# The last group's fourth maximum subtracted on TensorE, and a residual sum with a block maximum one tile later in the fill

## What is computed

```
x = x + attention(ctx, layernorm(x))          # 8 heads of 16; softmax over 64 keys
x = x + ffn(layernorm(x))                     # h = silu(xq @ Wg) * (xq @ Wu);  y = hq @ Wd
```

## Time and profile before

| | |
|---|---|
| median of 3 runs | 199.22 us (198.94 to 199.98) |
| the profiled execution, its own time | 199.67 us |
| its span, first to last instruction | 197.9 us (1.77 us lie around it) |
| busy in the span | PE 183.7, DVE 177.3, POOL 142.0, ACT 132.2 us |
| attention part | up to about 112 us |
| fill, tiles 0 to 7 | about 112 to 130 us |
| steady loop | about 130 to 187 us |
| drain | 187 to 197.9 us |

### The profile page before, as it was taken

One profiled execution on the slowest core, in us unless ns is written; L12 is line 12 of the kernel. 1 busy time (PEld: TensorE's weight loads), 2 busy tenths in 40 slices (PEclk: granted clock), 3 DMA queues, 4 the chain that ended last, 5 costly groups with the idle time before them and its releaser, 6 DMA issues.

```text
span 197.9 us, 5833 instructions
## 1 busy us (share of the span) xinstructions
PE 183.7 (93%) x2097; PEld 141.2 (71%) x2097; DVE 177.3 (90%) x394; ACT 132.2 (67%) x281; POOL 142.0 (72%) x208
## 2 busy tenths in 40 slices
PE   5979999999899999999998999789999998999884
PEld 5546876859659688597785776467778686778783
DVE  6539997899999999999979998999999989999971
ACT  3046999959769699696877846385476473766661
POOL 6333785566697897984928496797999975877891
PEclk9999999999999999999999999999999999999999
DMA  5799990400200000000000000000101010101005
GB/s 192 239 246 298 387 296 15 158 6 19 91 3 2 3 3 3 2 0 5 3 3 0 5 0 0 0 5 2 53 0 53 3 53 0 53 5 55 0 0 164
DMA packets 13699, 12.00 MB, mean 61 GB/s; under 512 B 790, under 2 KB 10590, under 8 KB 13670
## 3 DMA queue, kind: packets, MB, share of 16 engines
q1 hardware_dynamic: 13086, 11.23, 18.1%
q10 hardware_dynamic: 584, 0.39, 0.6%
HBM read 9.52 MB, written 2.10 MB: 59 GB/s over the span
## 4 chain that ended last, share of the span: by engine, by line
PE 55%; POOL 17%; issue 11%; DVE 7%; DMA 4%; ACT 2%; SPq 1%; POOLq 0%; DVEq 0%; ACTq 0%
PE bank L1065 7%; PE bank L1156 5%; PE bank L1053 5%; POOL wq_y L397 5%; DMA x_all<-in_x 4%; POOL hq L412 3%; PE bank L1028 3%; PE bank L1124 3%; PE bank L1121 3%; PE bank L1016 3%; PE a_pair L1016 3%; PE bank L1136 3%; PE bank L1002 3%; PE bank L1059 3%; POOL xn L284 2%
## 5 line engine op out<-in xcount | busy, mean ns | idle before, releaser
L1156 PE MATMUL bank<-wdT,hT 128*128 128x128 f32 x186 | 26.4, 278 | 1.8 <-issue 0.8
L1121 PE MATMUL bank<-guT,xqT 128*128 128x352 f32 x64 | 24.5, 464 | 1.8 <-DVE hh L875 1.8
L1156 PEld LDWEIGHTS bank<-wdT,hT 128*128 128x128 f32 x186 | 23.2, 191 | 3.1 <-issue 1.9
L1124 PE MATMUL bank<-guT,xqT 128*128 128x352 f32 x64 | 24.2, 460 | 0.0
L412 POOL TENSOR_TENSOR hq<-wq_u,sch 128x704 f32<-128x704 f32 x15 | 21.2, 1413 | 3.6 <-DVE wq_u L901 3.5
L397 POOL TENSOR_TENSOR wq_y<-hh,ivh 128x704 f32<-128x704 f32 x15 | 21.1, 1409 | 2.9 <-ACT ivh L632 2.3
L737 DVE TENSOR_REDUCE den<-prob 128x8 f32<-128x512 f32 x32 | 19.8, 663 | 0.0
L626 ACT COPY hT<-bank 128x384 f32<-128x384 f32 x32 | 15.2, 474 | 5.1 <-PE bank L1136 5.1
L1065 PE MATMUL bank<-wsT,cT 128*128 128x128 f32 x128 | 17.2, 278 | 0.1
L1136 PEld LDWEIGHTS bank<-ident,hq 128*128 128x128 f32 x96 | 11.9, 141 | 7.4 <-issue 3.0
L1136 PE MATMUL bank<-ident,hq 128*128 128x128 f32 x96 | 15.8, 274 | 1.5 <-POOL hq L412 0.9
(11 more groups left out here) (138 smaller groups left out, 506.0 us busy)
## 6 DMA issues: line engine op xcount, KB each, us to landing
cT<-in_ctxT SPq DMA_DIRECT2D x8, 512.0 KB, 5.4
x_all<-in_x SPq DMA_DIRECT2D x8, 256.0 KB, 6.4
mask_bc<-in_mask_rows SPq DMA_DIRECT2D x8, 256.0 KB, 6.5
out_y<-mask_bc SPq DMA_DIRECT2D x7, 256.0 KB, 2.2
wsT<-in_WsT ACTq DMA_DIRECT2D x1, 256.0 KB, 5.0
out_y<-mask_bc SPq DMA_DIRECT2D x1, 192.0 KB, 2.0
w_all<-in_wg SPq DMA_DIRECT2D x1, 176.0 KB
w_all<-in_wu SPq DMA_DIRECT2D x1, 176.0 KB
```

The lines of the kernel that those rows point to most:

```text
L1121: nc.tensor.matmul(gu_bank[2 * n % 3][:, 0:I], xqT[g % 2][:, t], guT[:, 0, :], start=True, stop=True).then_inc(pe_g, 1)
L1124: nc.tensor.matmul(gu_bank[(2 * n + 1) % 3][:, 0:I], xqT[g % 2][:, t], guT[:, 1, :], start=True, stop=True).then_inc(pe_u, 1)
L1156: last = nc.tensor.matmul(bank[:, j * P:(j + 1) * P], hT[n % 2][:, c, :], wdT[:, c, :], start=(c == 0), stop=(c == 2))
```

## The change

Three edits. In the last group (step k = 8) pair 3 is treated as the other pairs: TensorE subtracts its maxima in the bank with one more product behind that of pair 2, VectorE's subtraction is gone, and `exp` waits for `pe_mm` and reads the bank. And `x2_add(7)` with `block_max(6)` moves on VectorE from m = 4 to m = 5, behind that m's h_product(5), h_max(2) and h_reciprocal(2).

```diff
 exp(g, p):
-                if p == SUB:
+                if p == SUB and g < NG - 1:
                     act.wait_ge(sub_ok, g + 1)
                     nc.scalar.activation(pr, pr, ACT.Exp, scale=float(HD) ** -0.5).then_inc(p_ok, 1)
                     return
 VectorE, attn_step(k):
-                if on(g2):
+                if on(g2) and k < NG:
                     minus_max(g2)
                 if on(g4):
                     block_max(g4)
 VectorE, loop over m:
-                if m == 4:
+                if m == 5:
                     x2_add(NG - 1)
                     block_max(NG - 2)
 TensorE, attn_step(k):
                     minus_max(g2, 2)
+                    if k == NG:
+                        minus_max(g2, SUB)
                     prob_transpose(g2, 0)
                     prob_transpose(g2, 1)
```

## The result

| | before | changed |
|---|---|---|
| median | 199.22 us (10 runs, 198.75 to 200.64) | 201.66 us (10 runs, 200.28 to 203.38) |
| the profiled execution, its own time | 199.67 us | 201.09 us |
| its span | 197.9 us | 198.6 us |
| mean granted clock in the span | 1.000 | 0.991 |

What follows compares the result with a forecast made beforehand. The prediction took VectorE to set the pace from the end of the fill through half the steady loop. Its terms, 0 + 1.32 + 0.60 = 1.92 us, added to 199.22 gave 201.1 us, range 199.5 to 202.0.

Steps and rivals of the forecast that it cites:

- The first edit at zero: Last group's fourth maximum subtracted on TensorE: gain at the end taken as 0, capped at 0.06 us by h_product(1).
- block_max(6) 1.86 us late through GpSimd's queue: block_max(6) ends 1.86 us later, so GpSimd's scales, hq_unit(0), h_scales(2) and y_unit(2) all come 1.86 us later.
- 1.32 us at h_product(8): On VectorE at tile 8: silu(8) comes 1.86 us late, 0.57 us is slack, so h_product(8) starts 1.32 us later.
- TensorE's lateness as harmless: TensorE, 1.86 us late at h_transpose(0), has room to fall back into step with VectorE over the next tiles.
- 0.60 us at s3_round(6): VectorE arrives at 135.39 us while GpSimd's hq_unit(2) runs until 135.99, and waits the full overlap, 0.60 us.
- They follow each other without a gap: GpSimd's scales, hq_unit(0), h_scales(2) and y_unit(2) run back to back, so all are 1.86 us later.
- The row at 162.03: s3_round(7)'s second instruction in the kernel before: 1.76 us against a median of 0.72, blocked by an hq_unit until 163.23.
- The clock as a rival at 0.06: TensorE's clock falls to 1.2 GHz after some 3.4 us idle before h_transpose(0), giving 203.6 us; chance 0.06.
- The price of 2.5 us: Extra loss beyond the forecast if TensorE's clock falls: two tiles at half speed, about 2.5 us.
- The sum: Total delay on VectorE: 0 + 1.32 + 0.60 = 1.92 us, giving 201.1 us, 1.0% slower.
- the meeting: VectorE's s3_round(6) and GpSimd's hq_unit(2) overlap near 135 us and lock each other out, costing 0.60 us.
- VectorE as the bound: From 120.73 to 158.66 us VectorE, busy 37.13 of 37.93 us, sets the pace; delaying it delays the end.

Runs made afterwards that it cites:

- second measurement: The changed kernel timed once more, on the chip of its version with 26 useless products in TensorE's wait: ratio 1.0084 to the kernel before, median 201.59 us.
- e4_bmax_later: The kernel before with only block_max(6) moved to m = 5, x2_add(7) staying at m = 4: ratio 1.0120, or 2.4 us slower.
- e3_x2_later: The kernel before with only x2_add(7) moved to m = 5, block_max(6) staying at m = 4: ratio 1.0028.
- e6_after_scales: The changed kernel with GpSimd's scales2_of(6), which waits for block_max(6), put behind hq_unit(0), h_scales(2) and y_unit(2): ratio 1.0025 to the kernel before.
- e7_before_scales: The kernel before with GpSimd's scales2_of(6) put behind y_unit(2): ratio 0.9994.
- second trial: Second timing of the changed kernel with 26 useless products in TensorE's wait before h_transpose(0): ratio 1.0046 to the kernel before; the first timing gave 1.0011.

## Why the prediction was right

- **The first edit at zero.** Right at the end, where 0.05 us was measured. The cap at h_product(1) is a little looser than the 0.06 us worked out: the gate product of tile 3 starts 0.15 us sooner.
- **block_max(6) 1.86 us late through GpSimd's queue.** Right in kind. It is 1.76 us late, and so is h_transpose(0) (16.88 instead of 15.12 behind x2_add(6)), since VectorE was already 0.09 us ahead.
- **1.32 us at h_product(8).** With the clock up it is 1.22, by the way forecast, through silu(8), and so it is in one of the changed kernel's two traces (1.21). In the other it is 1.44, and TensorE's up product at half clock is the releaser. The text had TensorE's lateness as harmless.
- **0.60 us at s3_round(6).** Too large, and absent in both traces of the changed kernel. With the clock up it is 0.30, for two reasons. "They follow each other without a gap" failed: y_of(6) started 0.10 us behind the end of y_unit(2) before and starts right with it now, so hq_unit(2) is 1.60 us late and not 1.86, and the overlap is 0.38 us. And the loss is less than the overlap, since the instruction ends 0.55 us after GpSimd and not its full 0.63. The row at 162.03 shows that already: 1.20 us of overlap, up to 163.23, for a loss of 1.04. With the clock down VectorE arrives after GpSimd is done.
- **The clock as a rival at 0.06.** That chance was far too low. The clock is at 0.991 or lower in 7 of 10 executions of the changed kernel with the result and in 10 of 12 in its second measurement. The price of 2.5 us was too high by the traces: 0.2 us for some 3 us at half speed, 1.3 us for some 7 (the last h_product 2.87 us late in `e4_bmax_later`, 1.54 with the clock up).
- **The sum.** 1.92 was forecast, 1.9 timed (1.0094), 1.72 in the trace. That the total fits so well is in part luck: the path through GpSimd to VectorE carries 1.5 by the traces, with 1.22 + 0.30 where 1.32 + 0.60 stood, and in the changed kernel the clock took the place of the meeting. The forecast's direction, its first and larger term and the way that it takes are what the runs bear out.
- **VectorE as the bound.** Right: waits of TensorE and GpSimd removed in `e3_x2_later`, `e6_after_scales` and `e7_before_scales` changed nothing, 1.04 us removed from VectorE brought 1.2.

## What to carry to other kernels

Before a step is put later on one engine, look at the list of the engine that waits for its result: what costs is not the step but all that stands behind its wait. Here the cheap cure was to let the waiting instructions go behind work that was ready. Where an engine is the bound without gaps, first look for its instructions that last longer than others of their line: here one such row was worth more than any reordering of waits.

## What the runs showed of the hardware

- **TensorE's clock around a wait.** At waits of 2.74 and 3.18 us for hq the granted clock fell from 1.00 to 0.50, the level of 1.2 GHz, for some 3 to 7 us, and rose again while TensorE was at work. It fell within the wait of 2.74 us, and at the end of those of 3.18 or behind it. The same kernel does not always show it: 5 of 22 executions of the changed kernel have a mean clock of 1.00. With 26 small products in the wait (1.61 us), leaving 1.72 us idle, it stayed at 1.00 in all twelve executions of the second trial (three of the first show 0.998 or 0.999). A wait of 1.30 us left it at 1.00 in the kernel before.
- **VectorE and GpSimd at the port.** In these traces VectorE's instructions with two inputs in SBUF (s3_round) and GpSimd's products of 704 columns exclude each other: whichever starts first runs to its end, and the other ends 0.54 to 0.56 us (VectorE) or 1.24 to 1.25 us (GpSimd) after that. This fits the Trainium skill (SBUF — State Buffer, "SBUF: two separate sides"). The loss falls on the engine that comes second, and the order of the instructions can choose which one that is, or keep the two apart.
